# Two graph-attention layers and three residual blocks: one cast moved, filler products at the start, two vector steps swapped, and value sums in three 256-column products

## The reference

```python
def _gat_layer(x, W, adj):
    proj = x @ W
    Wh, Ws = jnp.split(proj, 2, axis=-1)
    scores = Wh @ Ws.T
    a = jax.nn.softmax(scores, axis=-1) * adj
    out = a @ Wh
    out = out + x
    return jax.nn.leaky_relu(out, NEG_SLOPE)

x = _layernorm(x + two _gat_layer in a row)                            # layers 1 and 2
x = _layernorm(x + relu(A_norm @ x @ W))                               # block 1, degree-normalised
x = _layernorm(x + relu(adj_norm @ x @ Wn.T + bn + x @ Ws.T + bs))     # block 2
x = _layernorm(x + adj @ (relu(adj @ (x @ W1) + b1) @ W2) + b2)        # block 3
```

## Time and profile before

| | us |
|---|---|
| median of three runs | 749.22 (748.46 to 749.93) |
| the profiled execution | 749.87 |
| its span on the core | 748.1 |
| TensorE busy in it | 720.9 |
| VectorE busy | 481.1 |
| ScalarE busy | 337.9 |
| GpSimd busy | 321.7 |

### The profile page before, as it was taken

How to read it: one execution, slowest core, us unless ns; L and a number is a source line. 1 busy time by engine, 2 the same in 40 slices (tenths; PEclk the granted TensorE clock), 3 DMA queues, 4 the chain that set the end, 5 groups by cost and what they waited for, 6 DMA issues and landing times.

```text
span 748.1 us, 13194 instructions
## 1 busy us (share of the span) xinstructions
PE 720.9 (96%) x3962; PEld 612.2 (82%) x3962; DVE 481.1 (64%) x1110; ACT 337.9 (45%) x785; POOL 321.7 (43%) x345
## 2 busy tenths in 40 slices
PE   6997999999999999999999999989999999999996
PEld 5886888888888888888888888878877787689985
DVE  3764777777777656465665665763677757875466
ACT  3754556656555565455565465451222412221112
POOL 0143676767676514645536445474665000003200
PEclk9998999999999999999999999999999999999999
DMA  7014233242423031433123232245762221210012
GB/s 266 29 57 169 85 124 130 94 158 84 162 92 112 29 127 57 103 120 130 71 88 122 70 99 112 71 101 126 185 182 90 71 63 57 71 43 3 1 43 73
DMA packets 63139, 72.39 MB, mean 97 GB/s; under 512 B 36336, under 2 KB 56432, under 8 KB 58992
## 3 DMA queue, kind: packets, MB, share of 16 engines
q1 hardware_dynamic: 63088, 71.78, 30.2%
HBM read 46.60 MB, written 16.78 MB: 85 GB/s over the span
## 4 chain that ended last, share of the span: by engine, by line
PE 87%; DVE 5%; issue 3%; ACT 2%; DMA 2%; POOL 1%; SPq 0%; DVEq 0%; POOLq 0%; ACTq 0%
PE scores L1891 37%; PE ob L1891 27%; PE tb L1891 9%; PE tb L2043 7%; PE xb L1891 3%; DMA keep<-in_x 1%; DMA arow<-in_adj 1%; PE tb L1987 1%; DVE zb L1668 1%; DVE norm_values L1674 1%; ACT prob L872 1%; PE xb L2068 1%; PE tb L1910 0%; DVE zb L1601 0%; PE xb L1933 0%
## 5 line engine op out<-in xcount | busy, mean ns | idle before, releaser
L668 POOL TENSOR_TENSOR prob<-prob,arow 128x512 f32<-128x512 f32 x128 | 189.9, 1506 | 151.4 <-ACT prob L872 151.3
L1891 PE MATMUL ob<-val,stationary 128*128 128x512 f32 x960 | 188.1, 346 | 0.0
L1891 PEld LDWEIGHTS ob<-val,stationary 128*128 128x128 f32 x960 | 147.9, 190 | 18.6
L1219 DVE TENSOR_TENSOR stationary<-tb,stationary 128x512 fp32r<-128x512 f32 x128 | 85.4, 687 | 59.7 <-ACT stationary L773 58.5
L1891 PE MATMUL scores<-wst_h,whs_h 128*128 128x512 f32 x256 | 102.7, 401 | 0.0
L1891 PE MATMUL scores<-wst_h,whs_l 128*128 128x512 f32 x256 | 100.0, 391 | 0.0
L1891 PE MATMUL scores<-wst_l,whs_h 128*128 128x512 f32 x256 | 99.8, 390 | 0.0
L1309 DVE TENSOR_REDUCE row_values<-scores 128x1 f32<-128x512 f32 x128 | 85.7, 682 | 13.2 <-PE scores L1891 11.9
L773 ACT ACTIVATE stationary<-tb 128x512 fp32r<-128x512 f32 x128 | 72.8, 594 | 45.3 <-PE tb L2043 43.8
L872 ACT ACTIVATE prob<-scores,row_values 128x512 f32<-128x512 f32 x128 | 86.7, 689 | 11.4 <-DVE row_values L1316 11.4
L2043 PE MATMUL tb<-ident,prob 128*128 128x128 f32 x512 | 72.7, 274 | 0.3 <-DVE stationary L1219 0.3
(11 more groups left out here) (224 smaller groups left out, 1202.0 us busy)
## 6 DMA issues: line engine op xcount, KB each, us to landing
arow<-in_adj SPq DMA_DIRECT2D x32, 1024.0 KB, 5.1
adjacency_halves<-arow SPq DMA_DIRECT2D x16, 512.0 KB, 3.0
features_scratch<-xs SPq DMA_DIRECT2D x32, 128.0 KB, 1.9
xres<-features_scratch SPq DMA_DIRECT2D x32, 128.0 KB, 2.2
keep<-in_x SPq DMA_DIRECT2D x4, 512.0 KB, 7.1
xres<-in_x SPq DMA_DIRECT2D x16, 128.0 KB, 2.0
self_term_scratch<-rst SPq DMA_DIRECT2D x16, 128.0 KB, 1.7
rin<-self_term_scratch SPq DMA_DIRECT2D x16, 128.0 KB, 2.2
```

The source lines that it names most:

```text
L668: nc.gpsimd.tensor_tensor(prob[u][:, cs], prob[u][:, cs], arow[u][:, cs], ALU.mult).then_inc(g.msk.sem, 1)
L1219: return nc.vector.tensor_tensor(dst, v, h.bitcast(F32), ALU.subtract)
L1891: return nc.tensor.matmul(o, l, r, start=start, stop=stop)
```

## The change

- ACT's cast of tile 1 in slot (0, 1) moves to before the exponentials, behind the first two chunks of hi.
- TensorE runs eight products of the identity with itself before features(0) and three after it, into a bank that nobody reads at that time. GpSimd casts the query half of the first layer's weights, ACT the other half. VectorE makes the low halves in the order feature 0, query weights, feature 1, other weights. project(0) starts after features(0) and takes each feature half as it comes, and features(1) is done between its second and its third output.
- In blocks 1 and 2 VectorE's residual stands ahead of rows_lo.
- attend does three products of 256 columns into one range instead of one of 512 and one of 256. ACT's lo_half and GpSimd's residual fall away: VectorE's scaled adds keep in the same step.
- At the end of layer 2, TensorE does attend of the last tile ahead of the next turn and of n_rows, and VectorE's n_moving stands two steps sooner.

```diff
-            copy(wg_h[:, :, :], wg_raw).then_inc(s_wgh[0], 1)
+            copy(wg_h[:, :, D:2 * D], wg_raw[:, :, D:2 * D]).then_inc(s_wgh[0], 1)
...
+            pool.wait_ge(s_wgraw[0], 16)
+            nc.gpsimd.tensor_copy(wg_h[:, :, 0:D], wg_raw[:, :, 0:D]).then_inc(s_wqh, 1)
...
-            features(0)
+            feature(0, 0)
+            dve.wait_ge(s_wqh, 1)
+            rest(wg_l[:, :, 0:D], wg_raw[:, :, 0:D], wg_h[:, :, 0:D]).then_inc(s_wgl[0], 1)
+            feature(0, 1)
             dve.wait_ge(s_wgh[0], 1)
-            rest(wg_l[:, :, :], wg_raw, wg_h[:, :, :]).then_inc(s_wgl[0], 1)
+            rest(wg_l[:, :, D:2 * D], wg_raw[:, :, D:2 * D], wg_h[:, :, D:2 * D]).then_inc(s_wgl[0], 1)
             features(1)
...
+            def keep_busy(n):
+
+                for _ in range(n):
+                    mm(xb0[:, 0:P], ident[:, :], ident[:, :], True, True)
+
+            keep_busy(8)
             features(0)
-            features(1)
+            keep_busy(3)
...
-                    rows_turned(i)
+                    if l or i:
+                        rows_turned(i)
                     for o in range(2 * KT):
-                        if not l and o == KT and i in (1, 2):
+                        if not l and o == KT:
                             features(i + 1)
+                            if i == 0:
+                                pe.wait_ge(s_wgl[0], 2)
...
                     if av:
                         hi(*p, 0)
                         hi(*p, 1)
+                    if first:
+                        cast_halves(b, u)
...
-                    if first:
-                        cast_halves(b, u)
...
-                    if av:
-                        lo_half(*p)
...
-                    nc.vector.scalar_tensor_tensor(zb[u][:, :], attention_bank(b, u)[:, 0:D], rinv[u][:, :], tmp[:, :],
+                    nc.vector.scalar_tensor_tensor(zb[u][:, :], attention_bank(b, u)[:, 0:D], rinv[u][:, :],
+                                                   keep[:, bass.ds(t, 1), :].rearrange("p a d -> p (a d)"),
                                                    ALU.mult, ALU.add).then_inc(g.z.sem, 1)
...
-                    if av:
-                        residual(*before(b, u))
...
                         if ep:
                             total(*p)
+                        if ep:
+                            residual(*p)
                         if fin:
                             rows_lo(*pp)
                         if ep:
-                            residual(*p)
                             norm(*p)
...
-                        mm(bank[:, 0:2 * D], ringh[c][:, qs], val[:, j, :], j == 0, False)
+                        mm(bank[:, 0:D], ringh[c][:, qs], val[:, j, 0:D], j == 0, False)
+                        mm(bank[:, 0:D], ringh[c][:, qs], val[:, j, D:2 * D], False, False)
                         last = mm(bank[:, 0:D], ringl[c][:, qs], val[:, j, 0:D], False, j == NT - 1)
...
+            attend(NT - 2, 1, 0)
             turn(NT - 2, 1, 2)
             n_rows(NT - 4, 0)
-            attend(NT - 2, 1, 0)
+            attend(NT - 2, 1, 1)
             turn(NT - 2, 1, 3)
-            attend(NT - 2, 1, 1)
```

More of the change, by code:

```diff
@@ L240, in adjacency_resnet @@
         s_wgh = [sem(f"gat_weight_hi_{l}") for l in range(LAYERS)]
+        s_wqh = sem("gat_query_weight_hi")
         s_wgl = [sem(f"gat_weight_lo_{l}") for l in range(LAYERS)]
@@ L286, in __init__ @@
                 self.rinv = s("row_sum_inverse", NT)
-                self.tmp = s("lo_half_scaled", NT)
                 self.z = s("attention_scaled", NT)
-                self.zx = s("residual_added", NT)
                 self.new = s("rows_ready", NT)
@@ L640, in widen @@
                     ge(pool, G[-1].msk, 4 * NT)
-                    ge(pool, G[-1].zx, NT)
+                    ge(pool, G[-1].z, NT)
                     pool.wait_ge(n_pl, NT)
@@ L669, in mask @@
                                                 ALU.mult).then_inc(g.msk.sem, 1)
[L671 to L675, removed]
                 def keep_rows(b, u):
@@ L873, in exp @@
                                          accum_out=rs[u][:, c:c + 1]).then_inc(g.ex.sem, 1)
[L875 to L880, removed]
                 def rows_hi(b, u):
@@ L980, in layer @@
                     hi(NT - 2, 1, 3)
-                    lo_half(NT - 2, 1)
-                return slot, hi, lo_half
+                return slot, hi
             last_layer = None
@@ L986, in _ @@
                 last_layer = layer(l, g, last_layer)
-            _, hi, lo_half = last_layer
+            _, hi = last_layer
             def keep_adj(t, c):
@@ L1219, in rest, with feature @@
                 return nc.vector.tensor_tensor(dst, v, h.bitcast(F32), ALU.subtract)
+            def feature(i, k):
+                dve.wait_ge(s_x0h, KT * i + k + 1)
+                gs = slice(i * CH, (i + 1) * CH)
+                rest(xtall_l[:, k, gs], tb[k][:, :], xtall_h[:, k, gs]).then_inc(s_x0l, 1)
             def features(i):
                 for k in range(KT):
-                    dve.wait_ge(s_x0h, KT * i + k + 1)
-                    gs = slice(i * CH, (i + 1) * CH)
-                    rest(xtall_l[:, k, gs], tb[k][:, :], xtall_h[:, k, gs]).then_inc(s_x0l, 1)
+                    feature(i, k)
             def weights():
@@ L1328, in row_sum @@
                     ge(dve, g.rsum, t + 1)
-                    ge(dve, g.tmp, t - 1)
+                    ge(dve, g.z, t - 1)
                     nc.vector.reciprocal(rinv[u][:, :], rsum[u][:, :]).then_inc(g.rinv.sem, 1)
@@ L1354, in scaled @@
                     t = b + u
-                    ge(dve, g.tmp, t + 1)
+                    ge(dve, g.av, 4 * t + 4)
                     ge(dve, g.rinv, t + 1)
                     ge(dve, g.new, t - 1)
-                    nc.vector.scalar_tensor_tensor(zb[u][:, :], attention_bank(b, u)[:, 0:D], rinv[u][:, :], tmp[:, :],
+                    nc.vector.scalar_tensor_tensor(zb[u][:, :], attention_bank(b, u)[:, 0:D], rinv[u][:, :],
+                                                   keep[:, bass.ds(t, 1), :].rearrange("p a d -> p (a d)"),
                                                    ALU.mult, ALU.add).then_inc(g.z.sem, 1)
@@ L1364, in finish @@
                     t = b + u
-                    ge(dve, g.zx, t + 1)
+                    ge(dve, g.z, t + 1)
                     if l == LAYERS - 1:
@@ L1543, in _ @@
             finish5(NT - 2, 0)
+            n_moving(NT - 4, 0)
             n_lo(NT - 3, 1)
             row_sum(NT - 2, 1)
-            n_moving(NT - 4, 0)
             n_inverse(NT - 2)
@@ L1905, in features @@
                     if i == 1:
-                        pe.wait_ge(s_x0l, k + 1)
+                        pe.wait_ge(s_x0l, KT)
                     elif i:
@@ L1943, in layer @@
             def layer(l, g, previous):
-                pe.wait_ge(s_wgl[l], 1)
-                if l:
-                    ge(pe, G[l - 1].ex, 4 * NT)
                 pe.sem_inc(g.prod.sem, 1)
@@ L1953, in layer @@
                 pe.sem_inc(g.vl.sem, 1)
+                pe.wait_ge(s_wgl[l], 1)
+                if l:
+                    ge(pe, G[l - 1].ex, 4 * NT)
                 def rows_turned(i):
@@ L1964, in project_part @@
                     gs, os = bass.ts(i, CH), slice(o * P, (o + 1) * P)
+                    if not l and isinstance(i, int) and i + o == 0:
+                        for k in range(KT):
+                            pe.wait_ge(s_x0l, k + 1)
+                            mm(bank[:, :], wg_h[:, k, os], xtall_h[:, k, gs], k == 0, False)
+                            mm(bank[:, :], wg_h[:, k, os], xtall_l[:, k, gs], False, False)
+                            last = mm(bank[:, :], wg_l[:, k, os], xtall_h[:, k, gs], False, k == KT - 1)
+                        last.then_inc(g.prod.sem, 1)
+                        return
                     exact3(bank[:, :], [(wg_h[:, k, os], wg_l[:, k, os], xtall_h[:, k, gs], xtall_l[:, k, gs])
```

## The result

The changed kernel takes 752.47 us (median of five, 751.77 to 752.80), the kernel before 749.03 (median of five in the same comparison). The ratio is 1.0039, 95% interval 1.0026 to 1.0053: slower by 0.39%, where 747.6 and a gain were forecast. The profiled execution of after took 752.47 with a span of 750.4, that of before 749.87 with 748.1.

What follows compares the result with a forecast made beforehand. TensorE, busy 96% of the span, was taken as the bound. Terms -3.1 - 7.7 + 2.0 - 1.1 + 8.3 = -1.6 us gave 748.3 for the profiled execution, 747.6 for the median; range 742.5 to 752.0.

Steps and rivals of the forecast that it cites:

- The head: Kernel start: earlier first projection with TensorE kept busy, values' first transpose at 14.55 instead of 17.66, -3.1 us.
- The second rival: Kernel start: the clock does not rise early, gain -1.1 instead of -3.1, 749.6 us in all; chance 0.15.
- The second cast: First layer, slot (2, 0): ACT's earlier cast removes TensorE's 5.01 us stall and the half clock after it, -7.7 us.
- Attention's sums: Both attention layers, 512 steps: three 256-column products instead of one of 512 and one of 256, +2.0 us.
- The layer ends: Ends of both attention layers: TensorE's waits for a split chunk and normalised rows shrink, -1.1 us together.
- the shorter tail: Layer ends: without ACT's scaled low half and GpSimd's residual, less work remains where no next tile hides it.
- VectorE's order: Blocks 1 and 2: residual ahead of the low rows closes a loop through projection and copy, +8.3 us.
- the start of block 1: Block 1's beginning: low rows wait behind a residual that hangs on a load, +1.6 us.
- The six intervals of block 1: Block 1's close projections: 27.22 us become 31.6 at a loop of 5.26 per tile, +4.3 us.
- the steady part: Steady tiles: TensorE's own 5.31 us per tile covers the loop of 5.26, so nothing shows.
- The first rival: Blocks 1 and 2: the reorder costs 0, or 4 us if half is regained; 739.3 or 743.3; chance 0.15.
- The third rival: Block 1: GpSimd slows VectorE's residual, loop 5.78 us; with full price of the sums 753.1 us; chance 0.13.

Runs made afterwards that it cites:

- without the fillers: Changed kernel without the eleven filler products (identity against identity, no reader) on TensorE at the head: 754.27 us over two runs.
- The cast alone: Kernel before with only ACT's second cast (tile 1's adjacency) moved ahead of the exponentials: 741.33 us over two runs, ratio 0.9895.
- old sums back: Changed kernel with the former attention products of 512 and 256 columns, ACT's scaled low half and GpSimd's residual restored: 748.43 us, ratio 0.9991.
- the two kernels with the old order: Changed kernel with VectorE's low rows again ahead of the residual in blocks 1 and 2: 742.22 us; with the former attention products too: 738.23 us.
- The run with the sharing products apart: Changed kernel with VectorE's former order, the low-half product placed between the two sharing the high stationary half: 743.27 us over two runs.
- the kernel with both parts back: Changed kernel with the former attention products and VectorE's former order in blocks 1 and 2: 738.23 us, ratio 0.9860.
- the kernel with the shorter loop: Changed kernel with only the adding of residual rows ahead of the low rows, statistics behind them: 743.45 us, ratio 0.9921.

## Why the prediction was wrong

**The head** was right in mechanism and size: first product 8.30 (8.05 forecast), values at 14.79 (14.55), -2.87. One profile fixes this term to about 1 us only: in the three kernels with the old head the values' first transpose starts at 16.40, 17.66 and 18.36, in the nine with the new one and its fillers at 13.96 to 14.79. The second rival, the late clock, did not come about: from the second product on the first projection's products stand 0.23 apart, and without the fillers the kernel is 1.8 slower.

**The second cast** was right: no stall, clock 1.00, -7.43 in a stretch that also holds some 0.2 of dearer sums. The cast alone shortens the way from the values' first transpose to the projection that ends layer 2 from 488.32 to 480.60: -7.72, with -7.7 forecast.

**Attention's sums** were mis-sized. +2.0 was taken; 3.57 was measured in the traces, and 4.0 by the medians (old sums back, and again between the two kernels with the old order, 742.22 and 738.23). The row of 0.120 per 256-column product in the earlier trace rows had the right price, 36 x 0.120 = 4.32 for twelve steps, and 4.31 was measured. The step that failed was to leave that row for a value between it and zero, on the ground that neighbours share a weight. The run with the sharing products apart shows that sharing is worth nothing here. The formula of the Trainium skill (TensorE: Matmul & The Clock Gate, Back-to-back issue gap), whose sum was given as +1.3, is stated there for an isolated product, and it is too cheap for this stream: the traces show 0.120 per product where it has 0.109.

**The layer ends** were right in sign only. Of the 2.72 by which the stretch to the end of layer 2 grew, the sums hold some 3.4 (3.57 less the 0.2 before 69.53), which leaves some -0.7. Two kernels with the old sums and the moved cast show it directly: before with the cast alone has 480.60 from the values' first transpose to the projection that ends layer 2, the kernel with both parts back 480.00. That is -0.6 where -1.1 was forecast. Both have the old, long tail, so the gain belongs to the new order at the end of layer 2, and the shorter tail, on which the forecast rested, gave nothing. The wait of 0.30 at the end of layer 1 that was to go is still there in after:

```profile
247.71 1.69 PE L1882 MATMUL scores<-val,stationary 128*128 128x256 f32 x12 [0.35 <-DVE stationary L1201]
```

**VectorE's order** was right in mechanism and 1.4 too small. VectorE's and ACT's timelines of after in block 1 show the loop as it was written out: low rows at 546.07, projection at 546.55, copy at 548.30, self term after 1.60 us of waiting, the next total.

```profile
546.07 0.42 DVE L1201 TENSOR_TENSOR xt_l<-scores,xt_h 128x256 fp32r<-128x256 f32 x1
...
548.30 0.39 ACT L766 ACTIVATE keep<-scores 128x256 f32<-128x256 f32 x1 [1.82 <-PE scores L1882]
...
548.77 0.42 DVE L1716 TENSOR_TENSOR rst<-scores,bsum 128x256 f32<-128x256 f32 x1 [1.60 <-ACT keep L766]
549.17 0.48 DVE L1591 SCALAR_TENSOR_TENSOR zb<-tb,dinv,rin 128x256 f32<-128x256 f32 x1
```

Term by term, from the starts above and in the earlier trace rows: the start of block 1, up to its second projection, +1.6 as forecast (26.82 from 498.40 to 525.22, against 25.19). The six intervals of block 1 took 31.90, +4.7 for 4.3; each was 5.32 where 5.26 had been added up. Block 2's took 25.79, +2.2 for 2.0, and its start +0.4 as forecast (from block 1's last projection to block 2's fourth, 25.23 against 24.83). The term that was missing is the steady part, +0.8. It was priced at nothing, because TensorE's own step of 5.31 seemed to cover a loop of 5.26. In after it did not: from 567.84 on the projections stand 5.40 apart. Rows of after and, below them, of before show why (PEld is TensorE's weight load):

```profile
569.33 1.09 PE L1882 MATMUL tb<-pm,adjr 128*128 128x512 f32 x4
570.55 0.48 DVE L1591 SCALAR_TENSOR_TENSOR zb<-tb,dinv,rin 128x256 f32<-128x256 f32 x1
572.75 0.42 DVE L1201 TENSOR_TENSOR xt_l<-xb,xt_h 128x256 fp32r<-128x256 f32 x1
573.23 0.19 PEld L1882 LDWEIGHTS scores<-w2h,xt_h 128*128 128x128 f32 x1 [0.27 <-DVE xt_l L1201]
573.24 0.49 PE L1882 MATMUL scores<-w2h,xt_h 128*128 128x512 f32 x1
573.57 0.39 PE L1882 MATMUL scores<-w2l,xt_h 128*128 128x512 f32 x1
```

```profile
574.08 0.19 PEld L1891 LDWEIGHTS scores<-w2h,xt_h 128*128 128x128 f32 x1
574.31 0.39 PE L1891 MATMUL scores<-w2h,xt_h 128*128 128x512 f32 x1
574.54 0.40 PE L1891 MATMUL scores<-w2l,xt_h 128*128 128x512 f32 x1
```

Before, the weights of a projection's first product were loaded 0.23 ahead of it, and the second product came 0.23 later. In after the load waits for the low rows and starts with the product, and the second product comes 0.33 later. The loop had been added up from a projection (584.93) whose products had not waited, so it lacked this 0.10. In the steady part, moreover, the total waits for TensorE's last four products of its tile, which stand behind the projection (569.33 + 1.09, then the total 0.13 later). So from a projection to the next total are 2.71 there (567.84 to 570.55) where 2.61 was taken; with 1.04 for the total, 1.16 for the residual and 0.49 for the low rows and their signal that makes 5.40. TensorE's own step of 5.31 grows by the same 0.10, so the margin was never there. In the kernel with the shorter loop the low rows end 0.8 ahead of the steady projections, and these stand 5.30 apart again.

**The first rival**, a reorder that costs nothing, is out: undoing it gains 10.25 us by the medians (9.96 in the traces, from the end of layer 2 to the last projection of block 2), doing it alone costs as much. **The third rival**, an adding slowed by GpSimd, is out as a mechanism: the adding of the residual rows took at most 0.60 in after and 0.43 in all but one tile of block 1, where before had up to 0.95, so the loop is 5.3 to 5.4 and not 5.8. That its 753.1 is the number nearest to the result is luck: the full price of the sums and the steady part that pays, which it held besides, came, the slowed adding did not.

The whole: -1.6 was forecast against the profiled execution, +2.6 came. Of the difference of 4.2, 1.6 are the sums, 1.4 the order, 0.5 the layer ends, 0.2 the head, and 0.5 the end of the span and what lies outside it. The sign was lost because gains of some 11 us stood against costs of nearly the same size, and the two large misses lay on the side of the costs. The range failed by 0.5 at its upper end: the bounds of the sums (+3.6) and of the order (+12) were named, but not allowed to come together. The median also moved by 3.4 rather than 2.6, because the profiled execution of before was itself 0.84 above its median.

## What to carry to other kernels

Before a step on an in-order engine is moved ahead of the one that releases the bottleneck, write out the loop that closes through the other engines and compare its length with the shortest interval between releases, not with the mean one; a margin of 1% (5.26 against 5.31) is no margin. Add such a loop up from rows in which its waits do occur: a row that had not waited can be shorter, here by 0.10. A row that has the price of an operation stands until a run shows another: don't discount it for a saving that no row shows. Where gains and costs cancel, change one part at a time: here the 11 us that two parts and the layer ends gained were given back by two others, and more.

## What the hardware showed

A product of 256 columns costs 0.120 us whether or not its neighbour shares its stationary half, one of 512 beside its 256-column partner 0.353 - 0.120 = 0.233: splitting one into two costs 7 ns a step, in either order of the products.

A projection whose low rows end just ahead of it starts more slowly, idle time or not. In all thirteen traces of this case the second product of a block 1 projection comes 0.30 to 0.35 after the first where the low rows ended at most 0.09 us before, and 0.22 to 0.24 where they ended at least 0.2 us before; in block 2 it is 0.21 to 0.23 against 0.11 to 0.12.

Which of VectorE and GpSimd comes first decides who is slowed. Before, in seven of block 1's sixteen tiles the adding of the residual rows on VectorE started behind GpSimd's self loop and took 0.87 to 0.94; the self loop took 0.74 in the median. After, VectorE comes first in nearly every tile: it takes 0.43 at most there, and the self loop, which starts about 0.13 behind it, takes 0.88 in the median. The lines of the adding hold block 2 too, which has no self loop, so their medians hide this. One line of each view, before (first two) and after:

```profile
L748 POOL TENSOR_TENSOR rin<-pm x16: 730/738/882, 516.4 to 583.4; 128x256 f32<-128x256 f32 x16
```

```profile
L1668 DVE SCALAR_TENSOR_TENSOR zb<-zb,xres x32: 412/416/945, 521.4 to 671.9; 128x256 f32<-128x256 f32 x32
```

```profile
L741 POOL TENSOR_TENSOR rin<-pm x16: 735/883/891, 508.7 to 582.5; 128x256 f32<-128x256 f32 x16
```

```profile
L1658 DVE SCALAR_TENSOR_TENSOR zb<-zb,xres x32: 414/425/599, 513.6 to 674.0; 128x256 f32<-128x256 f32 x32
```

(Durations in ns, shortest, median, longest.) The Trainium skill, SBUF — State Buffer, section Who interferes with whom, says that a VectorE instruction with two inputs in SBUF contends with GpSimd's reads for a shared port pair, and that issue order decides who blocks. The four lines agree: VectorE loses up to 0.53 behind GpSimd, GpSimd 0.15 behind VectorE. So the new order did take the conflict off VectorE, but the loop was too long even without it.
